# A gated recurrence on one core: both halves of r·h scanned ahead of the update gate's first sum, and the candidate's first chunk multiplied in one piece

## What is computed

```
def step(h, xs):
    xzt, xrt, xht = xs
    z = jax.nn.sigmoid(xzt + h @ U_z + vz)
    r = jax.nn.sigmoid(xrt + h @ U_r + vr)
    hh = jnp.tanh(xht + r * h @ U + vh)
    h_new = (1.0 - z) * h + z * hh
    return (h_new, h_new)
...
_, out_t = jax.lax.scan(step, h0, xs)
```

## Time and profile before

| what | us |
|---|---|
| median of 3 runs | 5889.6 |
| lowest and highest | 5885.95, 5890.36 |
| the profiled execution | 5891.46 |
| its span in the profile | 5889.6 |

### The profile page before, as it was taken

The page is one execution under the profiler, slowest core; times in us unless marked ns, Lnnn a source line. Parts: engine busy times, 40 slices in busy tenths (PEclk is TensorE's granted clock), DMA queues, the critical chain, the costliest instruction groups (busy, mean ns, idle before and its releaser), DMA issues.

```text
span 5889.6 us, 511092 instructions
## 1 busy us (share of the span) xinstructions
PE 5771.7 (98%) x200328; PEld 5619.0 (95%) x200328; DVE 5308.2 (90%) x47287; ACT 4158.3 (71%) x29549; POOL 8.3 (0%) x32
## 2 busy tenths in 40 slices
PE   8999999999999999999999999999999999999999
PEld 8999999999999999999999999999999999999999
DVE  5999999999999999999999999999999999999998
ACT  3777777777777777777777777777777777777776
POOL 0000000000000000000000000000000000000000
PEclk8999999999999999999999999999999999999999
DMA  3000000000000000000000000000000000000000
GB/s 92 21 20 20 21 20 21 21 18 20 21 21 20 21 18 21 20 21 20 20 21 20 21 21 18 21 20 21 20 21 18 21 21 20 20 20 21 20 21 20
DMA packets 80318, 130.01 MB, mean 22 GB/s; under 512 B 12336, under 2 KB 18480, under 8 KB 80304
## 3 DMA queue, kind: packets, MB, share of 16 engines
q1 hardware_dynamic: 80304, 129.81, 6.4%
HBM read 20.46 MB, written 8.65 MB: 5 GB/s over the span
## 4 chain that ended last, share of the span: by engine, by line
PE 89%; DVE 9%; issue 1%; ACT 0%; DVEq 0%; POOL 0%; POOLq 0%
PE quad L298 53%; PE pair_z L298 26%; PE ps_p L261 9%; DVE quad L577 3%; DVE h_part L621 1%; DVE z_fac L613 1%; DVE z_fac L607 1%; DVE rh_part L595 0%; PE pair_z L249 0%; ACT r_term L411 0%; DVE pair_z L577 0%; DVE oT L651 0%; DVE h_fac L644 0%; DVE h_safe L647 0%; DVE y_next L543 0%
## 5 line engine op out<-in xcount | busy, mean ns | idle before, releaser
L298 PE MATMUL quad<-h_part,u_part 128*128 128x48 f16 (+1 forms) x65568 | 2038.8, 183 | 91.3 <-DVE h_part L621 85.5
L298 PEld LDWEIGHTS quad<-h_part,u_part 128*128 128x128 f16 x65568 | 1847.4, 96 | 241.3 <-DVE h_part L621 198.9
L298 PE MATMUL quad<-rh_part,u_part 128*128 128x48 f16 (+1 forms) x65536 | 1994.0, 182 | 0.1
L298 PE MATMUL pair_z<-h_part,u_part 128*128 128x48 f16 (+1 forms) x65552 | 1940.5, 182 | 0.0
L577 DVE TENSOR_REDUCE quad<-quad 128x2 f32<-128x4 f32 (+1 forms) x12290 | 1866.2, 166 | 59.2 <-PE quad L298 18.2
L298 PEld LDWEIGHTS quad<-rh_part,u_part 128*128 128x128 f16 x65536 | 1844.9, 96 | 0.3 <-ACT quad L394 0.2
L298 PEld LDWEIGHTS pair_z<-h_part,u_part 128*128 128x128 f16 x65552 | 1785.8, 96 | 0.0
L621 DVE TENSOR_TENSOR_SCAN h_part<-z_fac,n_term 128x20 f16<-128x20 f32 x8192 | 1514.2, 196 | 2.0
L419 ACT ACTIVATE n_term<-quad 128x4 f32<-128x4 f32 x8192 | 1336.2, 172 | 117.9
L411 ACT ACTIVATE r_term<-quad 128x8 f32<-128x8 f32 x4098 | 581.2, 184 | 1178.7 <-DVE quad L577 1178.7
L394 ACT ACTIVATE quad<-xp 128x8 f32 (+2 forms) x6146 | 1040.8, 183 | 34.0 <-issue 31.6
(11 more groups left out here) (80 smaller groups left out, 1943.6 us busy)
## 6 DMA issues: line engine op xcount, KB each, us to landing
w_stage<-w_in SPq DMA_DIRECT2D x384, 256.0 KB, 2.3
x_tok<-in_x SPq DMA_DIRECT2D x68, 128.0 KB
out_dram<-o_tok SPq DMA_DIRECT2D x66, 128.0 KB, 2.3
mlp_w<-in_L_cond_W SPq DMA_DIRECT2D x2, 1024.0 KB, 6.7
u_raw<-in_L_cond_U_r SPq DMA_DIRECT2D x1, 1024.0 KB, 5.8
u_raw<-in_L_cond_U_z SPq DMA_DIRECT2D x1, 1024.0 KB, 7.8
u_raw<-in_L_cond_U SPq DMA_DIRECT2D x1, 1024.0 KB, 10.5
w_in<-in_L_cond_W_r SPq DMA_DIRECT2D x4, 256.0 KB, 9.8
```

The costliest lines, as they stand in the source:

```text
L298: return nc.tensor.matmul(to, u_part[:, g, part, k, m * P:(m + 1) * P], parts[:, at:at + run].unsqueeze(1).broadcast_to([P, repeats, run]) ...
```

## The change

VectorE does the second rh scan right behind the first, and z0's total behind both. TensorE does all 8 tiles of h's chunk 0 first, without the two tiles of chunk 1 in their midst, and waits for `seeds_in` in front of chunk 1. Nothing is added or removed.

```
                 early, late = range(HC), range(HC, K)
                 pe.wait_ge(s["rh0"], t1)
                 tiles(H, [0], early)
-                pe.wait_ge(s["seeds_in"], t1)
-                tiles(H, [1], early[:1])
                 pe.wait_ge(s["rh1"], t1)
                 tiles(H, [0], late, closes=True).then_inc(s["h0_mm"], 1)
-                tiles(H, [1], early[1:])
-                tiles(H, [1], late, closes=True).then_inc(s["h1_mm"], 1)
+                pe.wait_ge(s["seeds_in"], t1)
+                tiles(H, [1], range(K), closes=True).then_inc(s["h1_mm"], 1)
...
                 gated(0)
+                gated(1)
                 dve.wait_ge(s["z0_mm"], t1)
                 total(pair_z[:, 0:1], Z, HS, "z0_sum")
-                gated(1)
```

## The result

| | median us | runs | ratio to before |
|---|---|---|---|
| before | 5889.05 | 20 (5884.73 to 5890.36) | |
| changed | 5897.26 | 20 (5890.0 to 5899.99) | 1.0013, 95% interval 1.0007 to 1.0019 |

The kernel became slower by 8.2 us, between 4 and 11 by the interval. The prediction said 5913, 23 us more than before, and put 69% on slower by over 0.2%. The sign was right, and the range of 5884 to 5945 holds the time, but the size was off by a factor of nearly three, and by the bound of 0.2% the result belongs to "no change", which had 24%.

The account below looks back on a forecast made before the run. The prediction took a ring of dependent hand-offs through each step, with TensorE as a link, to bound the kernel. z0's total 15 us plus branch 8 us gave 23 us more, 5913 as a median, range 5884 to 5945.

Parts of the forecast that it names:

- The ring: Inner steps' closed chain: r tiles, totals, scans, z0's total, sigmoid, factors, inverse, h1's total, tanh, seed, tanh h2; 0.01 a step.
- Candidate: Second rh scan 0.06 earlier but wanted 0.05 earlier by TensorE: gain of 0.00 to 0.01 in a step.
- z0's total: Moved behind the second scan, 0.12 to 0.13 later; r tiles end 0.01 later in 1536 steps: 15 us, ends 0 and 31.
- Branch: VectorE's loop branch ahead of z1's total in u = 0 pays 0.02, 416 times: 8 us, ends 0 and 30.
- The later wait for seeds: TensorE's wait for seeds moves away from its path and costs nothing; given no gain.
- The sentence on the queue of 8: VectorE takes z0's total in while both scans are ahead, so the branch would cost about 416 x 0.01 = 4 us.
- Rival A: Not slower: z path has 0.02 more slack, below 0.01 delay at the 5th r tile; 5878 to 5898; chance 0.28.
- Rival B: Two scans in a row do not overlap, candidate ends 0.05 later: 77 us, 5970 and above; chance 0.08.
- Rival C: Branch pays in full, 0.07 or more 416 times: 45 us in all, 5935; 0.22 together with the terms' upper ends.

Follow-up runs that it names:

- the inverse's swap: Changed kernel with z's first inverse moved behind h1's total on VectorE: 5855.72, ratio 0.9955; once more: 5857.04, ratio 0.9951.
- the extra copy: Changed kernel with an unused small copy on VectorE between the second rh scan and z0's total: 5988.28, ratio 1.018.
- the pair with and without TensorE's half: Both with z's first inverse behind h1's total and VectorE's new order: 5857.04 with TensorE's new tile order, 5868.17 with its old one.
- the one with extra transposes: Changed kernel with 32 idle transposes on TensorE ahead of the first real one: 5890.49, ratio 1.0007.
- The swap alone: Kernel before with only z's first inverse moved behind h1's total: 5891.76, ratio 1.001.
- one half: Kernel before with only VectorE's new order, both rh scans ahead of z0's total; TensorE in the old order: 5898.25, ratio 1.0025.
- the other: Changed kernel with VectorE put back in the old order, so only TensorE's new tile order remains: 5965.73, ratio 1.0142.

## Why the prediction was right in its mechanism and wrong in its size

**The ring.** It was named rightly: z0's total, sigmoid, factors, inverse, h1's total, tanh. Adding 0.06 to its first link adds 0.06 to every step, and cutting it in its middle gives back 36 us. One link was named wrongly. The prediction let tanh h1 act only through tanh h2 and the 5th r tile. It also acts on the first r tile, 0.11 behind its end, where `n1_in` stands beside the wait for the new state.

**Candidate: 0.00 to 0.01 gained.** The second scan starts 0.13 behind the first as forecast, but it takes 0.19, not 0.21, and ends 0.02 earlier than I had it. In u = 1, where nothing else has moved, the r and z tiles come where they came before and the 9th candidate tile starts 0.021 earlier. The gain was real and twice what I gave it. In the changed kernel another ring holds the steps, and the gain does not make them shorter, but it keeps them from growing more: with the new state's scan no earlier, the next first r tile would by my estimate come 0.01 later than it does (next paragraphs). In the kernel with the inverse's swap it is what remains: 2.767 instead of 2.785.

**z0's total: 0.12 to 0.13 later, 15 us.** It comes 0.107 later against the first scan: the second scan holds VectorE for 0.11, not 0.12 or 0.13. On the other side the inverse starts 0.21 behind its factors, not 0.19, so two misses cancel in part. Counted from a step's first r tile, the next links came nearly as forecast: factors 0.085 later, h1's total and tanh h2 0.03 to 0.04 later, the 5th r tile 0.03 later, the 9th only 0.006 later, the last r tile 0.012 later.

The term was mis-sized all the same. This step failed: it took the later end of the r tiles as a cost of every step. But the next step's first r tile now starts 1.972 behind this step's last instead of 1.979, 0.007 earlier, and most of the 0.012 is won back there. The new state's scan allows that: it starts 0.01 earlier in the step, since the candidate does. From last r tile to last r tile the steps u = 1 to 3 are 0.003 to 0.004 longer, not 0.01. The rounds as a whole lost 13.1 us, but about 6 of them are the stall at the 5th r tile of u = 0, which was in no term. One of its 158 rounds in the changed kernel, tanh h2 and the 5th tile's weight load:

```profile
3006.16 0.16 ACT L417 ACTIVATE n_term<-quad 128x4 f32<-128x4 f32 x1
...
3006.42 0.10 PEld L298 LDWEIGHTS quad<-h_part,u_part 128*128 128x128 f16 x1
```

The tanh ends at 3006.32 and the tile starts 0.10 behind it instead of 0.05. The stretch from the last r tile of u = 4 to that of u = 0 is 0.03 or 0.05 longer in such rounds than in the others. So the ring's share is about 7 us.

**Branch: 8 us.** This step failed. From the end of sigmoid r1 to z1's total in u = 0, the timeline of before and of the changed kernel:

```profile
3007.07 0.18 ACT L411 ACTIVATE r_term<-quad 128x8 f32<-128x8 f32 x1
```

```profile
3007.54 0.18 ACT L409 ACTIVATE r_term<-quad 128x8 f32<-128x8 f32 x1
...
3007.78 0.19 DVE L593 TENSOR_TENSOR_SCAN rh_part<-h_fac,r_term 128x28 f16<-128x28 f32 x1
3007.89 0.15 DVE L575 TENSOR_REDUCE pair_z<-pair_z 128x4 f32<-128x8 f32 x1
3008.32 0.17 DVE L575 TENSOR_REDUCE pair_z<-pair_z 128x4 f32<-128x8 f32 x1 [0.28 <-PE pair_z L298]
```

Before, the sigmoid ends at 3007.25 and z1's total starts at 3007.86, 0.61 later. Changed, 3007.72 to 3008.32, 0.60. The median over the rounds is 0.597 in both, and 0.593 with the extra copy in line. The trace also has a record of the branch itself: it stands 0.12 behind the sigmoid's end in both kernels, z1's total starts 0.473 behind it in both, and in the changed kernel it stands 0.05 ahead of the start of z0's total, so it does not wait for that instruction. The branch is paid from the moment at which the last semaphore in front of it is satisfied; how many instructions wait in VectorE's line does not matter up to the three or four seen here. I had asked the right question and leaned to the right end, and still gave it 8 us where it is 0. The sentence on the queue of 8 (the Trainium skill, page "Advanced Engine Details and Errata", section Engine Queue Depths) had the better number, 4, and the trace agrees with it as far as it goes.

**The later wait for seeds: no gain.** This step failed too. I looked only at a step u = 3. In the third step of a turn the seeds were late for the 5th tile: the tile in that place started 0.07 earlier in the changed kernel, and that step lost 0.045 of its length, 1.4 us in all. In u = 4 it would have given 0.03, as the pair with and without TensorE's half shows under the inverse's swap, but here the z ring took it.

**What no step had.** In a turn's first step TensorE stood still between its 7th and 8th r tile in the kernel before, though no wait is due there. The weight loads of before, the 7th tile and the 8th:

```profile
2980.02 0.10 PEld L298 LDWEIGHTS quad<-h_part,u_part 128*128 128x128 f16 x1
...
2980.19 0.19 PEld L298 LDWEIGHTS quad<-h_part,u_part 128*128 128x128 f16 x5
```

Changed, four neighbours there start within the usual 0.025 of each other:

```profile
2980.62 0.17 PEld L298 LDWEIGHTS quad<-h_part,u_part 128*128 128x128 f16 x4
```

The gap of 0.17 instead of 0.025 is gone, and the step became 0.13 shorter, 4 us over the 32 turns. Where this stall and the one at the 5th r tile would fall in the changed build could not be read from the trace of before. But I had not looked at the head of a turn at all beyond z1's total.

So of 23 us forecast, the ring gave about 7 of its 15 and the branch none of its 8. What else moved was in no term: 6 us more by the stall at the 5th r tile, 6 us less at the heads of the turns (4 of them the other stall), and 3.5 us less ahead of the loops and behind them. Together this is the 3.4 us between the two profiled executions. The stretch ahead of the loops I can't explain: the first r tile comes at 77.0 to 78.1 us in some profiles and at 80.0 to 80.5 in others, leaving out the one with extra transposes. These parts are as large as the ring's 7 and could have outweighed it, so that the sign came out right is in part luck. The medians differ by 8.2, the profiled executions by 3.4 (that of before lies 2.4 above its median, that of the changed kernel 2.4 below), and the rest stays unexplained.

Rival A priced the case of a hidden z path, and its range (5878 to 5898) holds the measured 5897. But its reason is refuted: tanh h2 and the 5th r tile come 0.03 later in a step, where it asked for less than 0.01, and what is added to z0's path passes into the steps whole. Rival B, two scans that do not overlap, is refuted by the start 0.13 behind. Rival C falls with the branch. The plain form of the rule on the pipe (the Trainium skill, page "VectorE: DVE Perf Modes", section The DRAIN you can't avoid), by which the second scan would have started at the first one's end, does not hold for these pairs. The same section adds that a next instruction that is not held starts earlier, which the prediction left out and which the trace agrees with (0.13 behind a scan that takes 0.22).

## What to carry to other kernels

When work is moved forward on an engine, follow what is moved back until it meets a wait that was already tight; here 0.06 gained on one operand was undone by 0.107 lost on another, and the cure (one more swap, behind the link that the delay reaches) took 36 us off. The swap alone, without the change, gained nothing. Read each kind of step in a rolled loop, not one of them: the first steps of a turn and of a round held 6 us each way that the inner steps did not show. And a step that ends its tiles later is not longer by as much, if the next one starts closer behind it. And change both sides of a hand-off together: one half here costs 15 us, the other 82, both 8, and both with the swap gain 28.

## What the runs showed of the hardware

- A scan right behind a scan starts 0.13 behind it, takes 0.19 instead of 0.22, and holds VectorE for 0.11 instead of 0.13. So the second of a pair is cheaper than the first.
- Hand-offs have steady prices here: 0.03 to 0.04 between VectorE and ScalarE, 0.05 from a scan to the TensorE tile behind it, but 0.11 from tanh h1 to the first r tile, where TensorE has two semaphores to pass and takes the first with an instruction of its own.
- VectorE's loop branch costs 0.60 (median) from the last semaphore ahead of it to the next instruction that it starts, and nothing more for instructions that wait in line in front of it.
- TensorE can stand still with nothing left to wait for, in some builds and not in others: at one place of a turn the gap between two tiles is 0.10 to 0.18 us on the mean instead of 0.025, and at the 5th r tile of u = 0 the tile comes 0.02 to 0.05 later than usual behind the tanh that it waits for. In the changed kernel the first took 4 us off and the second added 6, each about as much as the change's own 7.
